# A selective-scan and expert-layer kernel: one sum moved behind its step's other matmuls, the group turn two steps earlier, a rearranged first expert

## What is computed

```python
h = adaptive_layernorm(x, language)            # per-sequence weights
for i in range(4):                             # four state-space layers
    h = mamba_block(layer_norm(h), ...) + h    # d_inner 256, 16 states
x = x + h
y = gated_experts(x)      # dense: 8 experts and a shared one, all on all tokens
# sparse layer on y: softmax router, top 2 of 8 experts, 1024 slots each
h = gelu(disp @ w_gate[e]); eo = h @ w_down[e]
out = x + g1 * eo[slot1] + g2 * eo[slot2]
```

## Time and profile before

| | |
|---|---|
| Median of 3 runs | 2632.39 us (2632.32 to 2633.63) |
| Profiled execution, its own time | 2634.35 us |
| Its span, first to last instruction | 2632.6 us |
| TensorE granted clock, mean | 0.948 of full |
| Busy: PE, DVE, ACT, POOL | 2342.5, 2078.1, 1561.9, 2067.2 us |

### The profile page before, as it was taken

One profiled execution on the slowest core, in us unless ns is written; L12 is line 12 of the kernel. 1 busy time (PEld: TensorE's weight loads), 2 busy tenths in 40 slices (PEclk: granted clock), 3 DMA queues, 4 the chain that ended last, 5 costly groups with the idle time before them and its releaser, 6 DMA issues. The chain is left out here.

```text
span 2632.6 us, 22468 instructions
## 1 busy us (share of the span) xinstructions
PE 2342.5 (89%) x5996; PEld 1039.8 (39%) x5996; DVE 2078.1 (79%) x2044; ACT 1561.9 (59%) x2432; POOL 2067.2 (79%) x1287
## 2 busy tenths in 40 slices
PE   6688998889898989999999999999998899999594
PEld 4233333333333333333333333333333344444373
DVE  4799999999999999999999999999999443333221
ACT  3677777777776677767666767666765223222221
POOL 4599999999998799999999999999999332321266
PEclk9799999999999999999999999999999899999797
DMA  7466445654455766676666666666676500100363
GB/s 219 187 212 217 169 159 200 210 204 142 150 184 197 250 234 231 230 233 222 229 225 232 223 230 227 225 224 232 229 233 214 161 21 9 37 9 9 87 122 35
DMA packets 216928, 464.94 MB, mean 177 GB/s; under 512 B 29468, under 2 KB 109154, under 8 KB 216802
## 3 DMA queue, kind: packets, MB, share of 16 engines
q1 hardware_dynamic: 204818, 455.30, 51.3%
q0 software_dynamic: 11264, 7.98, 2.0%
q10 hardware_dynamic: 720, 0.23, 0.0%
HBM read 440.00 MB, written 23.99 MB: 176 GB/s over the span
## 5 line engine op out<-in xcount | busy, mean ns | idle before, releaser
L893 DVE TENSOR_TENSOR_SCAN hh<-decays,psdB 128x1024 f32<-128x1024 f32 x512 | 1165.1, 2282 | 56.7 <-ACT decays L715 18.7
L1037 POOL TENSOR_TENSOR products<-hh,Clo 128x1024 f32<-128x1024 f32 x408 | 977.1, 2398 | 113.3 <-DVE hh L893 110.9
L452 PE MATMUL psY<-products,ident 128*128 128x512 f32 x1640 | 797.6, 608 | 93.9 <-POOL products L1037 51.0
L715 ACT ACTIVATE decays<-dt,Acur 128x508 f32<-128x508 f32 x1024 | 667.8, 708 | 2.6 <-DVE hh L893 2.2
L452 PEld LDWEIGHTS psY<-products,ident 128*128 128x128 f32 x1640 | 307.0, 193 | 514.7 <-issue 350.2
L882 DVE TENSOR_TENSOR psdB<-psT,Blo 128x1024 f32<-128x1024 f32 x395 | 483.9, 1225 | 29.4 <-ACT psT L683 2.5
L1041 POOL TENSOR_TENSOR products<-products 128x512 f32<-128x512 f32 x204 | 258.8, 1269 | 16.0
L1465 DVE TENSOR_TENSOR ac<-sg,d_bank 128x512 f32<-128x512 f32 x135 | 92.7, 687 | 225.5 <-PE d_bank L1315 179.2
L432 PE MATMUL psW<-xnT,wcur 128*128 128x512 f32 x496 | 227.9, 601 | 39.2 <-DMA diag<-diags_l 20.4
L1037 POOL TENSOR_TENSOR products<-hh,late 128x1024 f32<-128x1024 f32 x104 | 244.1, 2366 | 16.2 <-PE psY L452 16.2
L1363 ACT ACTIVATE sg<-d_bank 128x512 f32<-128x512 f32 x135 | 80.6, 597 | 244.7 <-PE d_bank L1311 241.5
(11 more groups left out here) (216 smaller groups left out, 3104.6 us busy)
## 6 DMA issues: line engine op xcount, KB each, us to landing
Blo<-rows SPq DMA_DIRECT2D x280, 512.0 KB, 6.1
Clo<-rows SPq DMA_DIRECT2D x280, 512.0 KB, 5.1
late<-rows SPq DMA_DIRECT2D x104, 512.0 KB, 6.9
wcur<-taps_l SPq DMA_DIRECT2D x31, 512.0 KB
fw<-in_Wg SPq DMA_DIRECT2D x36, 256.0 KB, 5.4
fw<-in_Wu SPq DMA_DIRECT2D x36, 256.0 KB, 4.5
fw<-in_Wd SPq DMA_DIRECT2D x36, 256.0 KB, 5.3
disp<-fw SPq DMA_DIRECT2D x16, 528.0 KB, 7.8
```

What stands on the lines that cost most here:

```text
L452: ins = pe.matmul(psY[:, :], lhsT=ident[:, :], rhs=gg[k % NGB][:, j, :], start=False, stop=(k % NK == NK - 1 and j == last - 1))
L715: ins = act.activation(dA[k % NDA][:, j, :, 1:T], dt[i % 2][:, c, :, 1:T], ACT.Exp, scale=Acur[i % 2][:, s:s + 1])
L893: dve.tensor_tensor_scan(out=hh[k % NHB][:, :, :].rearrange("p c t -> p (c t)"), data0=dA[k % NDA][:, :, :, :].rearrange("p c q t -> p (c ...
L1037: ins = pool.tensor_tensor(gg[k % NGB][:, :, :], hh[k % NHB][:, :, :], tile(Clo, Chi, slot(i, s)), ALU.mult)
```

## The change

- `SUM_FIRST` loses step 7: the sum of the eighth step now comes last in its step on PE, behind dt1.
- On ACT "dt1" is moved ahead of "sums0" in step 12.
- `T_AT` goes from 3 to 2, `X_AT` from 9 to 7, and SP's store in a turn iteration from step 4 to step 2.
- In the expert stage each expert has its own `home`, so `address` no longer waits for `added`; `eos` has three buffers, and that wait moves to `weigh` for experts 3 and up. For expert 0 PE does `up(0, 0)` and `down(0, 0)` before the second half's `up`, and DVE weighs the first half before it picks expert 1.

```diff
-SUM_FIRST = (7, 15)
+SUM_FIRST = (15,)
-          12: ["sums0", "dt1", "softplus"], 13: ["outT"], 14: ["added"], 15: ["centre", "dtu0"]}
+          12: ["dt1", "sums0", "softplus"], 13: ["outT"], 14: ["added"], 15: ["centre", "dtu0"]}
-T_AT, X_AT = 3, 9
+T_AT, X_AT = 2, 7
-                        if i % NF == (FIRST - 1) % NF and 0 <= d <= NDF and k == 4:
+                        if i % NF == (FIRST - 1) % NF and 0 <= d <= NDF and k == 2:
                             store_x(d)
...
-        NDX = 3
+        NDX, NEO = 3, 3
...
-        eos = [sb(f"eos{p}", [128, NCH, D]) for p in range(2)]
-        home = [sb(f"home{p}", [128, NCH], u32) for p in range(2)]
+        eos = [sb(f"eos{p}", [128, NCH, D]) for p in range(NEO)]
+        home = [sb(f"home{e}", [128, NCH], u32) for e in range(NE)]
                 turn(0, 0)
-                for e in range(NE):
+                up(0, 0)
+                turn(0, 1)
+                down(0, 0)
+                up(0, 1)
+                turn(1, 0)
+                down(0, 1)
+                for e in range(1, NE):
                     turn(e, 1)
                     up(e, 0)
                     up(e, 1)
                 def address(e):
                     dve.wait_ge(picked, CR + NHT * (e + 1))
-                    if e > 1:
-                        dve.wait_ge(added, 16 * NCH * (e - 1))
-                    dve.tensor_copy(home[p][:, :], dx[1][x][:, :, D]).then_inc(homed, 1)
+                    dve.tensor_copy(home[e][:, :], dx[1][x][:, :, D]).then_inc(homed, 1)
                 def weigh(e, c):
                     if c == 0:
                         dve.wait_ge(weighted, e + 1)
+                        if e >= NEO:
+                            dve.wait_ge(added, 16 * NCH * (e - NEO + 1))
                 for e in range(NE):
                     turned(e, 1)
                     address(e)
+                    if e == 0:
+                        weigh(e, 0)
                     if e + 1 < NE:
                         pick(e + 1, 0)
                         turned(e + 1, 0)
                         pick(e + 1, 1)
-                    weigh(e, 0)
+                    if e > 0:
+                        weigh(e, 0)
                     weigh(e, 1)
```

More of the change, by code:

```diff
@@ L1545, in _ @@
                 for e in range(NE):
-                    p = e % 2
                     pool.wait_ge(homed, e + 1)
@@ L1553, in _ @@
                             pool.wait_ge(evac, CR + h + 1 + (n % HC if last(h) else 0))
-                        pool.indirect_dma_start(tokens, bass.IndirectOffsetOnAxis(ap=home[p][:, n:n + 1], axis=0), eos[p][:, n, :], None,
+                        pool.indirect_dma_start(tokens, bass.IndirectOffsetOnAxis(ap=home[e][:, n:n + 1], axis=0), eos[e % NEO][:, n, :], None,
                                                 bounds_check=NSEQ * T - 1, oob_is_err=False, compute_op=ALU.add).then_inc(added, 16)
@@ L1625, in address @@
                 def address(e):
-                    p, x = e % 2, e % NDX
+                    x = e % NDX
                     dve.copy_predicated(dx[1][x][:, :, D + 2], K["first"][:, e, :], dx[0][x][:, :, D + 1]).then_inc(weighted, 1)
                     dve.wait_ge(picked, CR + NHT * (e + 1))
-                    if e > 1:
-                        dve.wait_ge(added, 16 * NCH * (e - 1))
-                    dve.tensor_copy(home[p][:, :], dx[1][x][:, :, D]).then_inc(homed, 1)
+                    dve.tensor_copy(home[e][:, :], dx[1][x][:, :, D]).then_inc(homed, 1)
                 def turned(e, c):
@@ L1639, in weigh @@
                 def weigh(e, c):
-                    h, p = NHT * e + c, e % 2
+                    h, p = NHT * e + c, e % NEO
                     if c == 0:
                         dve.wait_ge(weighted, e + 1)
+                        if e >= NEO:
+                            dve.wait_ge(added, 16 * NCH * (e - NEO + 1))
                     for lo, n in ((q, 1) for q in range(HC)) if last(h) else ((0, HC),):
```

## The result

The changed kernel takes 2638.07 us (median of 14 runs, 2636.42 to 2640.99) beside 2633.45 us (median of 14, 2630.9 to 2634.66) for the one before: ratio 1.0019, 95% interval 1.0012 to 1.0027. That is 5.0 us slower (3.2 to 7.1), where 1.4 us was forecast and 2633.8 us as the time: inside its range, and just within what the text called no change. The profiled span grew from 2632.6 to 2636.2 us, though TensorE's mean granted clock rose from 0.948 to 0.966. So PE was granted more speed and the kernel was slower.

A forecast was written before the change was run, and what follows sets the result against it. DVE, with PE and POOL nearly full, bounds the streaming part; POOL's chain bounds the last stage. Early 0, streaming +4.4, turn +0.8, experts −3.8 make +1.4: 2633.8 us against the median, range 2627 to 2639, 8 in 10 within 2619 to 2645.

The forecast's parts named there:

- Early iterations, 0 us: Early iterations: PE's steps 7 and 8 precede its wait for POOL's step 13 product, so nothing gained; ends 0 and +14.4.
- The rival of a low clock there: Early iterations: clock falls at the sum of step 12, 8.4 us for twelve iterations, 2642 us; chance 0.25.
- Streaming part, where the lead ends: PE's 4.9 us lead becomes 3.15 us idle before step 13's sum; low clock follows, step 15's sum no sooner.
- The rival of a clock that stays up: Streaming part: PE's lead is kept and the wave gains 8.6 us; total −11.6, 2620.8 us; chance 0.28.
- Its size, 1.4 us at x0 and +4.4 in all: Streaming part: low clock costs 1.4 us at x0; six floor iterations +5.4, three longest −1.0; +4.4 us, bounds −8.6 and +9.
- The floor of 0.9: DVE's wait for the up matmul with PE on time at sum 15; six of fifteen streaming iterations already there.
- Group turn, +1.2 per turn less 4.1: Four turns: idle time and transposes ahead of the up matmul cost 4.9 us, DVE waits going return 4.1; +0.8, ends −1 and +5.
- Expert stage, −3.8: Last stage: second expert starts 2.8 us sooner on POOL, collision with SP's load −1.0; −3.8 us, ends −6 and −1.
- The collision: Expert stage: SP's load of rows beside the last additions moves to the next expert: −3.1 and +2.0, together −1.0 us.
- What would show it: Signs: no idle before step 7's sum, about 3 us before step 13's, clock 0.50 behind, L493 waits 27–30, first addition near 2483.

The follow-up runs named there:

- e4_fill: e1_sum with three zero-weight matmuls on PE ahead of the sum of step 13 in streaming iterations: 2626.32 us, ratio 0.9965 to the kernel before.
- e1_sum: Kernel before with only the sum of step 7 last and dt1 ahead of sums0: 2634.77 us, ratio 1.0005 to the kernel before.
- e5_unpair: e1_sum with step 13's two states added by PE instead of POOL: 2613.27 us, ratio 0.9928 to the kernel before.
- e12_all_unpair: Whole change, group turn included, with step 13's two states no longer added on POOL: 2620.13 us, ratio 0.9943 to the kernel before.
- e9_unpair_expert: e5_unpair plus the expert-stage changes, without the group turn: 2608.73 us, ratio 0.9894 to the kernel before.
- e2_turn: Kernel before with only the group turn's edits (transposes, copy back and store sooner): 2634.16 us, ratio 1.0003 to the kernel before.
- e10_unpair_old_order: e9_unpair_expert with the sum of step 7 and the dt1 copy in their old order: 2642.69 us, ratio 1.0032 to the kernel before.

## Why the prediction was right or wrong

**Early iterations, 0 us: right.** The waits are 16.2 us again, and the rival of a low clock there (2642 us) fell. The idle times were forecast at 2.5 and 1.8 us and came as 2.20 and 1.54.

**Streaming part, where the lead ends: right.** No idle time before the sum of step 7, 2.88 us in place of 3.15 before that of step 13, 0.50 granted at x0 or just ahead of it, and the sum of step 15 no sooner than before. `e4_fill` shows the cause: take away the low clock and 10.5 us come back. The rival of a clock that stays up (2620.8 us) fell. The Trainium skill's page "TensorE: Matmul & The Clock Gate", section "HAM oscillation — how this bites in real kernels", counts only longer gaps as harmful. The trace does not agree: 2.8 to 2.9 us were enough in 11 of 15 iterations.

**Its size, 1.4 us at x0 and +4.4 in all: right in the usual place, short beside it.** In the rows shown PE takes 8.7 us from the sum of step 13 to that of step 15 (1326.0 − 1317.35), 1.8 more than the 6.87 of before. So DVE's wait behind it does not stay but grows by 0.35 us (1.88 to 2.23). In `e1_sum` the fifteen waits before the scan of step 5 are 28.1 us in place of 24.0, so +4.1. What the text did not count are four waits before the scan of step 2, 3.4 us, each behind a low stretch that took 2.8 to 3.1 us and not 1.4, and on the other side the 2.6 us in turn iterations, which are gone. Sum of the waits: +4.9 us; by the length of the streaming part +3.7, by the timed runs +1.3.

**The floor of 0.9: read from PE's side alone.** "No reordering ahead of sum 15 can give more" than 8.6 us was true of PE's order with POOL as it was. The floor was POOL's addition at step 13, and it was worth 9.8 us more in `e5_unpair` by the timed runs and 15.8 by the streaming part.

**Group turn, +1.2 per turn less 4.1: the step that failed.** The 1.2 came: 0.76 us idle, then the transposes; and the waits before the scan of step 5 are +10.0 us in the whole change, where the two parts were given 4.4 + 4.9. But the 4.1 us in return were credited to the turn as if it alone could earn them. The 2.6 us of small waits in turn iterations are gone in `e1_sum` already; with the turn added only the wait for `psT` is left to gain, 1.5 to 0.6 us, and the new waits before the scan of step 2, 2.3 us in the whole change, take the place of the old. So the return was 2.6 − 2.3 + 0.9 = 1.2 us, 2.9 less than forecast. Streaming part and turn together: 10.0 − 1.2 = +8.8, by the length of the streaming part +7.8 to +8.1, by the timed runs +7.1, where the text had +5.2. The turn alone costs 0.8 us by the timed runs, as forecast, but 2.4 by the streaming part; with the sum moved it costs 5.8 and 4.4.

**Expert stage, −3.8: −2.4.** The first addition came 3.6 us sooner, just below the 3.9 to 5.6; the four up matmuls were granted 0.62 of the clock on average and took 5.93 us in place of 3.60. The stage as a whole, to the end, is 2.5 us shorter (160.2 against 162.6). The second came 1.4 sooner, not 2.8: its weighing was forecast at 2499.6 to 2501.3 and stands at 2501.83 on the old start. The collision moved one expert on, as forecast, with 5.82 us.

**The total.** The time lies inside the range by 0.9 us (2638.07 against 2639). The turn was put too low and the expert stage's gain too high, so these two errors add. The sum part, forecast at 4.4, came as 3.7 us by the streaming part and 1.3 by the timed runs, which took some of that back; so far it was luck that the range held.

**What would show it.** L493 near 27 to 30 us did not come: 31.5 in the sum part and 36.3 in the whole. The first addition near 2483 did: 2490.19 less the 6.0 us that the stage starts later is 2484.2.

## What to carry to other kernels

A lead given to one engine can be lost where it next has to wait: to the clock that falls in the idle time, and to the engine that it waits for. Here the new order alone was worth nothing. Filling the idle time gave 9 us. POOL's relief with the old order cost 8 us, yet with the new order (and the expert part in both) it gave 28. So before judging an edit by itself, ask who holds the place where its gain ends, and try both. Where two edits put work ahead of the same instruction, their prices are not those of each alone. And a timed difference of a few us over a whole kernel can come from a stage that no edit touched: the length of the stage itself, read from its first and last rows, tells.

## What had not been expected

The low clock does not follow from the length of the idle time alone. In `e12_all_unpair` PE idles 1.45 to 1.54 us before the sum of step 13 in 16 iterations, and 6 of these sums run at half speed; in `e9_unpair_expert` 1.45 to 1.53 us come 12 times, and none does. In iteration 21 even the rows ahead are the same, as the time line of PE in `e9_unpair_expert` shows:

```profile
1368.96 1.88 PE L452 MATMUL psY<-products,ident 128*128 128x512 f32 x4
1371.11 1.12 PE L493 MATMUL psdB<-late,fw 128*128 128x512 f32 x2 [0.26 <-DVE late L920]
1373.76 1.98 PE L452 MATMUL psY<-products,ident 128*128 128x512 f32 x4 [1.53 <-POOL products L1037]
```

In `e12_all_unpair` these three stand 1.85 us later, with the same durations and idle times but for the last, which takes 3.45 us. What decides between them stays open; the runs show only that the same pattern at another moment can have another clock. The three zero-weight matmuls took 2.79 us of otherwise idle time and kept the clock up in all iterations. Why DVE waits 6.4 and 5.2 us for loads of `Blo` in `e2_turn` and `e10_unpair_old_order`, 1.6 us before and not at all after the change, was not found.
